# The end of a fused two-block kernel: a bank of its own for each last gate and each output, and the output loop written out

## The reference, cut to what matters

```python
def _L1_ffn_ref(x, wf, uf, bf, wi, ui, bi, wc, uc, bc, wo, uo, bo, in_c):
    def step(c, xt):                       # one step per batch b: 8 steps, one cell of 512 x 128
        ft = sigmoid(xt @ wf.T + c @ uf.T + bf)
        it = sigmoid(xt @ wi.T + c @ ui.T + bi)
        gt = tanh(xt @ wc.T + c @ uc.T + bc)
        return ft * c + it * gt, None
    c_final, _ = lax.scan(step, c0, x)
    return tanh(einsum('tbi,oi->tbo', x, wo) + c_final @ uo.T + bo)
...
h = _layernorm(x) * (1 + cb) + sb          # x after the attention's residual
x = x + gb * _L1_ffn_ref(h, ...)           # the output
```

## Time and profile before

| | us |
|---|---|
| median of three runs | 2014.01 (2011.98 to 2016.75) |
| the profiled execution, whole | 2007.07 |
| its span, first to last instruction | 2005.0 |
| attention's last value matmuls end | 1953.26 |
| `op` of the last batch, PE | 1955.21 to 1957.27 |
| `z4T`, PE | 1962.17 to 1963.27 |
| the three last gates, PE and ACT | 1964.12 to 1974.16 |
| the last cell ready | 1976.67 |
| output loop, first matmul to last DVE operation | 1976.92 to 2002.13 |

### The profile page before, as it was taken

One profiled execution on the slowest core, in us unless ns is written; L12 is line 12 of the kernel. 1 busy time (PEld: TensorE's weight loads), 2 busy tenths in 40 slices (PEclk: granted clock), 3 DMA queues, 4 the chain that ended last, 5 costly groups with the idle time before them and its releaser, 6 DMA issues.

```text
span 2005.0 us, 38499 instructions
## 1 busy us (share of the span) xinstructions
PE 1817.2 (91%) x10716; PEld 1079.4 (54%) x10716; DVE 1271.0 (63%) x3791; ACT 1172.3 (58%) x3575; POOL 675.8 (34%) x697
## 2 busy tenths in 40 slices
PE   5676699999999989999999999999999999999995
PEld 3333455655555555555565555555555556555552
DVE  5999576566566656665656656665666565666672
ACT  3564356666566656665666656665656566666661
POOL 0565613333334323332333333432333233333300
PEclk8787799999999999999999999999999999999998
DMA  4001111121111201111112111120111111211101
GB/s 158 1 0 27 25 49 38 39 52 48 37 41 39 53 18 47 37 40 48 38 38 52 48 36 41 39 53 21 44 37 39 48 38 39 51 48 38 38 1 42
DMA packets 71351, 81.55 MB, mean 41 GB/s; under 512 B 29520, under 2 KB 37840, under 8 KB 70992
## 3 DMA queue, kind: packets, MB, share of 16 engines
q1 hardware_dynamic: 71120, 78.76, 15.9%
HBM read 7.91 MB, written 2.10 MB: 5 GB/s over the span
## 4 chain that ended last, share of the span: by engine, by line
issue 49%; PE 21%; POOL 18%; DVE 9%; ACT 2%; POOLq 1%; DMA 0%; DVEq 0%; SPq 0%; ACTq 0%
PE bank L1856 6%; PE bank L1883 3%; PE bank L1816 3%; POOL arena L696 3%; POOL arena L698 2%; POOL arena L695 2%; POOL arena L683 2%; POOL arena L682 2%; PE bank L1709 2%; DVE arena L1244 1%; POOL arena L694 1%; POOL arena L734 1%; PE bank L1704 1%; PE bank L1779 1%; PE bank L1762 1%
## 5 line engine op out<-in xcount | busy, mean ns | idle before, releaser
L1455 DVE CUSTOM_DVE_ANT_0 arena<-bank,W 128x512 f32<-128x512 f32 (+3 forms) x1024 | 480.7, 488 | 520.5 <-PE bank L1856 338.1
L1017 ACT ACTIVATE arena<-arena 128x512 f32<-128x512 f32 (+3 forms) x1024 | 570.3, 559 | 380.3 <-DVE arena L1455 376.3
L1856 PE MATMUL bank<-arena 96*128 96x512 f32 (+6 forms) x2048 | 719.8, 454 | 14.2 <-issue 14.2
L1856 PEld LDWEIGHTS bank<-arena 96*128 96x128 f32 x2048 | 352.4, 193 | 190.1 <-issue 152.9
L1883 PE MATMUL bank<-W,arena 128*128 128x128 f32 x2560 | 430.5, 282 | 0.4 <-ACT arena L1017 0.4
L1883 PEld LDWEIGHTS bank<-W,arena 128*128 128x128 f32 x2560 | 301.2, 144 | 225.4 <-issue 182.4
L1466 DVE COPY arena<-bank 128x512 f32<-128x512 f32 (+1 forms) x512 | 318.6, 622 | 89.2 <-PE bank L1883 86.5
L734 POOL TENSOR_TENSOR arena<-arena,one 128x512 f32<-128x512 f32 x64 | 66.5, 1039 | 834.5 <-DVE arena L1423 828.2
L1816 PE MATMUL bank<-arena 128*32 128x256 f32 (+1 forms) x3072 | 228.6, 362 | 2.8 <-issue 2.0
L1017 ACT ACTIVATION_READ_ACCUMULATOR arena<-arena 128x1 f32 x1024 | 197.1, 192 | 0.0
L996 ACT ACTIVATE arena<-bank 128x384 f32<-128x384 f32 x256 | 124.4, 486 | 98.3 <-PE bank L1883 96.4
(11 more groups left out here) (254 smaller groups left out, 2188.5 us busy)
## 6 DMA issues: line engine op xcount, KB each, us to landing
arena<-arena SPq DMA_DIRECT2D x896, 64.0 KB, 2.0
arena<-arena SPq DMA_DIRECT2D x64, 128.0 KB, 2.4
W<-wide SPq DMA_DIRECT2D x1, 3730.0 KB, 13.3
X<-x SPq DMA_DIRECT2D x8, 256.0 KB, 5.8
out<-arena SPq DMA_DIRECT2D x8, 256.0 KB, 2.3
arena<-arena SPq DMA_DIRECT2D x96, 16.0 KB, 1.9
LW<-lat SPq DMA_DIRECT2D x1, 768.5 KB, 14.3
arena<-mods SPq DMA_DIRECT2D x1, 768.0 KB, 4.6
```

What stands on the lines that cost most here:

```text
L1017: done = A(here, here, ACT.Exp, bias=nmax[:, c:c + 1], scale=-1.0, accum_out=lsum[:, c:c + 1])
L1455: last = v.tensor_tensor_reduce(Pb[:, s % 4, at_p:at_p + n], bank[turn.score_bank(s)][:, at + lo:at + lo + n], w("mask", T - n), -1.0, 3e3 ...
L1856: last = MM(B_[:, at:at + lo + n], query(t), Kb[a][g % 2][0:QD, h, skip:skip + lo + n], start=True, stop=True)
```

## The change

The gates of the last batch leave the task list. Each gets a bank that the scores have left (0, 1, 2): its product with the old cell is issued ahead of its product with the new input, the first two ahead of `op`, the third behind it. ACT reads them behind a semaphore of their own (`s_tg`, `s_tga`), and DVE's `cell_forget` waits for the first of them alone.

Each output has a bank (`out_bank`), in which its product with `HT`, its product with the cell and, once ACT has read it, its transposes come one after the other. The eight products with `HT` stand ahead of the wait for the last cell: those of outputs 0 to 3 ahead of `z4T`, those of 4 to 7 behind the gates. The loops of the four engines are written out, and PE does the transposes of output b - 2 behind the cell product of output b; DVE has the same order. `ho` and `hg` get four places, and with `ob` they move to another part of the arena.

```diff
-TAIL = ["op", "z4T", "gf", "gi", "gc"]
+TAIL = ["op", "z4T"]
...
         cv = Carve()
-        ho = cv(2, T)
-        hg = cv(2, T)
+        cv.at = own
+        ho = cv(4, T)
+        hg = cv(4, T)
         ob = cv(B, NT, P)
+        out_bank = (3, 4, 5, 6, 7, 0, 1, 2)
...
-            with sp.Fori(0, B // 2) as i:
-                for e in range(2):
-                    sp.wait_ge(s_ob, i * 2 + e + 1)
...
+            for b in range(B):
+                sp.wait_ge(s_ob, b + 1)
+                sp.dma_start(o_v[:, b], ob[:, b]).then_inc(s_st, 16)
...
+            for n, (gate, bias, scale) in enumerate(((gf, hbf, 0.5), (gi, hbi, 0.5), (gg, vec("bc"), 1.0))):
+                act.wait_ge(s_tg, n + 1)
+                A(gate, bank[n][:], ACT.Tanh, bias=bias, scale=scale).then_inc(s_tga, 1)
+
+            for b in range(B):
+                act.wait_ge(s_op, b + 1)
+                if b >= 4:
+                    act.wait_ge(s_hg, b - 3)
+                A(ho[:, b % 4], bank[out_bank[b]][:], ACT.Tanh, bias=vec("bo")).then_inc(s_ho, 1)
...
-            cell_forget(turn)
+            cell_forget(s_tga, 1)
+            v.wait_ge(s_tga, 3)
             cell_new(cell_sum(cell_input()))
...
+            def out_gated(b):
+                v.wait_ge(s_ho, b + 1)
+                if b >= 4:
+                    v.wait_ge(s_oT, b - 3)
+                TS(hg[:, b % 4], ho[:, b % 4], modc[:, 11, b:b + 1], None, ALU.mult).then_inc(s_hg, 1)
+
+            def out_added(b):
+                v.wait_ge(s_oT, b + 1)
+                TT(ob[:, b].rearrange("p j c -> p (j c)"), X[:, b * T:(b + 1) * T], bank[out_bank[b]][:], ALU.add).then_inc(s_ob, 1)
+
+            for b in range(B + 2):
+                if b < B:
+                    out_gated(b)
+                if b >= 2:
+                    out_added(b - 2)
...
+            def gate_past(n, name):
+                MM(bank[n][:], w(f"u{name}T"), c_st, start=True, stop=False)
+
+            def gate_now(n, name):
+                MM(bank[n][:], w(f"w{name}T"), HT[:, (B - 1) * T:], start=False, stop=True).then_inc(s_tg, 1)
+
+            def out_first(b):
+                MM(bank[out_bank[b]][:], w("wo2T"), HT[:, b * T:(b + 1) * T], start=True, stop=False)
+
+            def out_cell(b):
+                MM(bank[out_bank[b]][:], w("uoT"), c_st, start=False, stop=True).then_inc(s_op, 1)
...
```

More of the change, by code:

```diff
@@ L503, in build @@
         s_c = sem("cell_ready")
+        s_tg = sem("last_gates_in_psum")
+        s_tga = sem("last_gates_read")
         s_op = sem("out_in_psum")
@@ L617, in _ @@
             o_v = out_d.rearrange("b (j p) c -> p b j c", p=P)
-            with sp.Fori(0, B // 2) as i:
-                for e in range(2):
-                    sp.wait_ge(s_ob, i * 2 + e + 1)
-                    sp.dma_start(o_v[:, ds(i * 2 + e, 1)].rearrange("p b j c -> p (b j) c"), ob[:, ds(i * 2 + e, 1)].rearrange("p b j c -> p (b j) c")).then_inc(s_st, 16)
+            for b in range(B):
+                sp.wait_ge(s_ob, b + 1)
+                sp.dma_start(o_v[:, b], ob[:, b]).then_inc(s_st, 16)
             sp.wait_ge(s_st, 16 * B)
@@ L1365, in normed_out, with cell_forget @@
                 made.then_inc(s_z4, 1)
-            def cell_forget(turn):
-                v.wait_ge(s_ga, turn.read("gc"))
+            def cell_forget(seen, count):
+                v.wait_ge(seen, count)
                 step(STT(gf, gf, 1.0, c_st, ALU.add, ALU.mult))
@@ L1520, in attend @@
                         if at == 21:
-                            cell_forget(turn)
+                            cell_forget(s_ga, turn.read("gc"))
                         if at == 22:
@@ L1924, in _ @@
             attend(last_turn)
-            for name in TAIL:
-                fill(last_turn, name, NG - 2 if name == "op" else 0)
-            pe.wait_ge(s_c, B + 1)
[L1928 to L1936, removed]
+            def gate_past(n, name):
+                MM(bank[n][:], w(f"u{name}T"), c_st, start=True, stop=False)
@@ new lines, in gate_now, with out_turned @@
+            def gate_now(n, name):
[4 more added lines that the diff above has]
+                MM(bank[out_bank[b]][:], w("uoT"), c_st, start=False, stop=True).then_inc(s_op, 1)
+            def out_turned(b):
+                pe.wait_ge(s_hg, b + 1)
+                for j in range(NT):
+                    last = pe.transpose(bank[out_bank[b]][:, j * P:(j + 1) * P], hg[:, b % 4, j * P:(j + 1) * P], ident)
+                last.then_inc(s_oT, 1)
@@ new lines, in _ @@
+            all_units, all_rows = B * NG * GU, B * NG * GR
+            pe.wait_ge(s_p, all_units)
+            pe.wait_ge(s_c, B)
+            gate_past(0, "f")
+            gate_past(1, "i")
+            fill(last_turn, "op", NG - 2)
+            gate_past(2, "c")
+            out_first(0)
+            out_first(1)
+            pe.wait_ge(s_nrm, all_rows)
+            out_first(2)
+            pe.wait_ge(s_iv, all_rows)
+            out_first(3)
+            fill(last_turn, "z4T", 0)
+            pe.wait_ge(s_ga, last_turn.read("z4T"))
@@ L1939 @@
+            for n, name in enumerate(("f", "i", "c")):
+                gate_now(n, name)
+            out_first(4)
+            for n in range(3):
+                pe.wait_ge(s_tga, n + 1)
+                out_first(5 + n)
+            pe.wait_ge(s_c, B + 1)
+            for b in range(B + 2):
+                if b < B:
+                    out_cell(b)
+                if b >= 2:
+                    out_turned(b - 2)
 STEPS_C, STEPS_POOL_A, STEPS_POOL_C = 31, 10 * B + 14, 44
```

## The result

The changed kernel took 1987.65 us in the median of four executions (1986.08 to 1990.68), the kernel before 2013.11 in the median of four (2011.98 to 2016.75). The profiled execution took 1986.08, its span 1984.1; the forecast for these two was 1986.6 and 1984.5. So the sum came out in the profile, and not in the difference of the medians. The experiments are about that gap as much as about the parts.

A forecast was written before the change was run, and what follows sets the result against it. No engine bounds the last 51.7 us; a chain of waits hands over between engines. Savings of 1.0, 0.44, 6.78 and 12.84 less 0.56 give 20.5 us, taken off the median 2014.01: 1993.5 us, range 1988 to 1998.5.

The forecast's parts named there:

- the sum: Over the kernel's end: savings of 1.0, 0.44, 6.78 and 12.84 us, less 0.56 for transfers, make 20.5 us.
- `op`: Task behind the last value matmuls: old-cell products ahead of it keep PE's clock up, 1.0 us saved of 2.06.
- `z4T`: Four transposes ahead of `HT`: at the full clock 0.66 us instead of 1.10, 0.44 saved.
- From `HT` to the first cell product: Gates and cell: PE, with seven products queued, starts the first cell product 6.06 us after `HT` instead of 12.84; 6.78 saved.
- Output part to the last addition: Output loop: PE the bound at 1.30 us an output, last addition ended at about 12.37 instead of 25.21; 12.84 saved.
- Covers: PE's idle times around `op`: 1.95 us hides two added products (1.72), 4.90 us hides five (4.30); no cost.
- I take the sum off the median: Last step: the 6.9 us between profile and median lie ahead of the change and stay, so 2014.01 becomes 1993.5 us.
- An early fall of the clock: Rival, 10%: the clock falls at `op` anyway and comes back later; span 1986.0, median 1995.0 us.
- The ring: Rival, 8%: output part held by its order and buffer places, not PE; about 1.6 us an output, 2.4 lost, 1995.9.
- No gain: Rival, 2%: the clock stays low from `op` to the end; span 2004.5, time 2013.5 us, no change.
- Loading of instructions: Rival, 2%: engines outrun the loader in the written-out end; nine stops of 2.3 us eat the gain, eleven give 2018.
- The clock, weighed: Clock at `op`: by the skill page the new kernel keeps it for certain; by the trace it may lose it.

## Why the prediction was right about the kernel and missed the median

**The sum, term by term.** In the first profiles the change took 51.7 to 31.3, 20.4 us; the sum said 20.5. `op`: 1.0 forecast, 2.06 to 1.14 measured. `z4T`: 0.44 forecast, 1.10 to 0.64. From `HT` to the first cell product: 6.06 forecast, 6.15 measured (1962.25 to 1968.40); PE was late for the cell by 0.63, forecast 0.6 before the wake-up. Output part to the last addition: 12.37 forecast, 12.27 measured, PE the bound at 1.31 an output for 1.30. From the last addition to the end: 3.43 both times. Covers held: the two products ahead of `op` cost nothing, the five behind it left PE waiting 0.62 for `z4T`, 0.60 forecast.

**The step that failed** is the last one, "I take the sum off the median", with its "the medians themselves move by 2 to 3 us, as the three runs do". Three runs within 4.8 us looked like a narrow spread. The executions of this kernel spread over 18 us (2002.1 to 2019.7 in 84), standard deviation 3.9, so a median of three or four moves by more than 2, the difference of two such by about 3.4 (an estimate from that deviation), and the profile that I summed against was itself one of the shortest draws, in its attention (1953.3 against a mean of 1957.5) and in its end (51.7 against 52.6). The reason given for that step, that the 6.9 us between the profile and the median lie ahead of the change and stay, was also wrong in part: 0.9 of them lay in the end. The difference by 21 and 84 executions is 22.6 with a standard error of 1.0 (chips not told apart): 2.1 over the sum and 2.9 under the first comparison. Of the 2.1 the four profiles of the old end explain 0.9; the rest is within the error. The mean of the 21, 1989.6, lies inside the forecast's range, 1988 to 1998.5, and the median of the first four, 1987.65, just under it: the range gave two medians of so few executions too little room.

**A term that was too small** is thus the clock. The sum took what the one profile showed at 1.2 GHz: `op`, `z4T` and the first gate, 3.4 us. Over four profiles it is 4.3, since in three of them the clock falls a second time ahead of the output loop, which it does in no profile of the changed kernel. I had read the row of that stretch, where the clock stayed at 1.00 through an idle time of over 3 us, as what the kernel does, and it was what one execution did. The profiled executions agreed (1986.08 us for 1986.6) because the attention had been short in both: it ended at 1953.3 and 1952.8, where the means are 1957.5 and 1956.3. That is luck; the agreement of the ends is not, since every profile of the changed kernel has the same 31.2 to 31.3.

**The rivals.** An early fall of the clock: in none of four profiles of the changed kernel; where the two products stood behind `op`, it came. The ring: refuted, cell products are 1.31 apart and the transposes never wait until the last output. No gain: refuted. Loading of instructions: no piece called "issue" above 0.14 us in the chain of the changed end. Against this rival the prediction also named the Trainium skill ("Runtime: NRT & Kernel Launch", section "Instruction fetch mechanics") and put it too shortly: the page has a taken branch stall only where its target is not among the two pages of instructions at hand. The 0.25 us ahead of the old loop show no such stall, and say nothing of a far branch.

**The clock, weighed,** set two readings against each other: the Trainium skill's ("TensorE: Matmul & The Clock Gate", section "HAM oscillation — how this bites in real kernels"), by which an end without long gaps keeps the clock for certain, and the trace's, by which it might lose it all the same. The page's forecast came true four times in four. But the rule behind it fails elsewhere: with the two products behind `op` PE's longest gap was 1.94 us, and the clock fell all the same. That a short gap can lose the clock and a long one keep it, as in the first profile, holds, and the other profiles of the kernel before show the same instructions with the clock lost ahead of `op`, behind it, and again ahead of the outputs.

**Which half of the change does what.** The output part is worth 16.6 us by itself, the gates 5.7, both 21.3. Of the 21.3, 4.3 are the clock, and 1.5 to 1.7 what writing out the loops gives. That share the prediction gave no number; it stood inside a sum that was right because the sum was built from engine times and not from the old loop's.

## What to carry to other kernels

Work that doesn't need the last value belongs into the waits in front of it, and it pays twice where the waiting engine is TensorE: its queue behind the wait is shorter, and it comes to that queue at the full clock. Sum such a change against the profile, stage by stage, and compare stages again afterwards; the end of the changed kernel came out within 0.1 us in four profiles, that of the old one, with its two clocks, within 1.7, while whole executions spread by 18. And before a sum is taken off a median, ask how the kernel's executions spread: three runs close together don't say.

## What the runs showed of the hardware that was not expected

The same instructions took 1680.1 us in one execution and 1691.8 in another, with mean granted clocks of 0.959 and 0.951 over the whole. Six executions of the changed kernel on one chip went from 1985.6 to 1999.4 us, those under 1993 at clocks of 0.954 to 0.956, those above at 0.950 and 0.951. So on a core that works by itself the clock granted to TensorE differs from execution to execution of one program, and with it goes the time, by 0.6% between the first two; what decides it is not shown.

Products that nobody reads, put into idle stretches, made an old end of 52.6 us one of 48.3 in two profiles out of two. And the hardware loops cost 0.34 us in each turn of two outputs: the delays stand between the arrival of an operation's input and its start on DVE, and at the start of a turn on PE, in a chain in which the engines hand over to each other.
